# The pair stage of a graph-attention kernel: three PSUM places dealt out anew, and head scaling moved from VectorE to ScalarE and GpSimd

## What is computed

```python
alpha = jax.nn.leaky_relu(score, negative_slope=ALPHA)      # ALPHA = 0.2
m     = segment_max(alpha.T, src);  ex = exp(alpha.T - m[src])
denom = segment_sum(ex, src)[src];  att = ex / (denom + 1e-16)
out   = segment_sum(att[:, :, None] * h_e[:, dst], src)     # 8 heads of 64
x     = x + out.reshape(N, 512) + mixer(xn)
x     = x + ffn(layernorm(x))
```

## Time and profile before

| | us |
|---|---|
| median of 3 executions | 1156.71 (1156.32 to 1156.78) |
| the profiled execution | 1153.63 |
| its span, first to last instruction | 1151.5 |
| the pair stage in it, first L1873 to the first f1 matmul | 937.6 to 1096.0 |

### The profile page before, as it was taken

One profiled execution on the slowest core, in us unless ns is written; L12 is line 12 of the kernel. 1 busy time (PEld: TensorE's weight loads), 2 busy tenths in 40 slices (PEclk: granted clock), 3 DMA queues, 4 the chain that ended last, 5 costly groups with the idle time before them and its releaser, 6 DMA issues.

```text
span 1151.5 us, 11896 instructions
## 1 busy us (share of the span) xinstructions
PE 1009.2 (88%) x4204; PEld 667.0 (58%) x4204; DVE 781.3 (68%) x1315; ACT 325.8 (28%) x569; POOL 358.7 (31%) x321
## 2 busy tenths in 40 slices
PE   7779997999989998999896997999859748888988
PEld 6765487644466444844453435776546427777854
DVE  8994496534477566855434378998987659898742
ACT  5682164322310224022113111321114204333401
POOL 5371800000020102001010126777777604344400
PEclk9979995999999998999897998999989867888999
DMA  9997020020410023001120315333333295422001
GB/s 295 307 309 238 0 100 1 1 91 14 171 43 1 1 91 102 35 0 52 46 109 1 118 39 162 94 96 100 102 94 94 66 417 199 178 90 79 18 1 44
DMA packets 65314, 115.07 MB, mean 100 GB/s; under 512 B 11393, under 2 KB 43393, under 8 KB 63341
## 3 DMA queue, kind: packets, MB, share of 16 engines
q1 hardware_dynamic: 56301, 93.08, 23.7%
q0 software_dynamic: 8960, 21.31, 6.6%
HBM read 85.88 MB, written 28.49 MB: 99 GB/s over the span
## 4 chain that ended last, share of the span: by engine, by line
PE 50%; DVE 23%; POOL 11%; issue 8%; DMA 7%; ACT 0%; DVEq 0%; SPq 0%; POOLq 0%
PE ps L717 21%; PE ps L853 8%; POOL arena L657 6%; PE ps L726 5%; DMA pairs<-arena,pairi 5%; PE ps L709 4%; DVE arena L1534 4%; POOL pairs L667 4%; DVE arena L1873 3%; PE ps L751 2%; PE ps L1029 2%; DMA arena<-pairs 2%; PE ps L903 2%; PE ps L1054 2%; PE ps L789 2%
## 5 line engine op out<-in xcount | busy, mean ns | idle before, releaser
L717 PE MATMUL ps<-arena 128*125 128x512 f32 x400 | 180.2, 606 | 0.0
L586 POOL TENSOR_TENSOR small<-small 125x1 f32<-125x1 f32 x50 | 35.5, 710 | 435.5 <-DVE small L1348 435.5
L709 PE MATMUL ps<-ident,arena 125*128 125x125 f32 (+3 forms) x545 | 85.2, 298 | 51.1 <-DVE small L1873 14.2
L717 PE MATMUL ps<-arena,xnT 128*125 128x512 f32 x280 | 126.0, 608 | 4.2 <-DVE x L1786 4.2
L717 PEld LDWEIGHTS ps<-arena 128*125 128x125 f32 x400 | 75.2, 193 | 89.9 <-issue 89.9
L709 PEld LDWEIGHTS ps<-ident,arena 125*128 125x128 f32 (+3 forms) x545 | 73.7, 175 | 83.1 <-issue 37.2
L936 PE MATMUL ps<-ex_low,high 125*125 125x512 f32 x400 | 107.8, 417 | 0.0
L1212 ACT ACTIVATE arena<-ps,cols 128x125 f32<-128x125 f32 x120 | 43.2, 467 | 214.2 <-PE ps L709 214.2
L667 POOL DMA_INDIRECT pairs<-arena,pairi x80 | 87.2, 1090 | 25.5 <-issue 25.5
L717 PEld LDWEIGHTS ps<-arena,xnT 128*125 128x125 f32 x280 | 53.6, 194 | 69.7 <-issue 69.3
L692 POOL TENSOR_TENSOR arena<-arena,counts 125x625 f32<-125x625 f32 x40 | 58.0, 1452 | 105.7 <-ACT arena L1317 92.0
(11 more groups left out here) (214 smaller groups left out, 1771.5 us busy)
## 6 DMA issues: line engine op xcount, KB each, us to landing
pairs<-fill SPq DMA_DIRECT2D x10, 2500.0 KB, 22.2
arena<-pairs SPq DMA_DIRECT2D x5, 2500.0 KB, 11.2
arena<-pairs SPq DMA_DIRECT2D x10, 1250.0 KB, 6.5
arena<-in_mw SPq DMA_DIRECT2D x6, 2048.0 KB, 8.7
arena<-in_rows SPq DMA_DIRECT2D x16, 250.0 KB
arena<-in_qkv_w SPq DMA_DIRECT2D x1, 3072.0 KB
arena<-in_cw SPq DMA_DIRECT2D x3, 1024.0 KB, 5.3
arena<-in_w_qkvT SPq DMA_DIRECT2D x1, 3072.0 KB
```

The costliest lines, as they stand in the source:

```text
L709: last = pe.transpose(slot[0:n, at:at + rows], src, ident[0:rows, 0:rows])
L717: last = mm(slot[0:m, lo:hi], lhsT_of(k), rhs_of(k)[:, lo:hi], start=(k == 0), stop=(k == ks - 1))
```

## The change

Four things change, all in this stage.

- The PSUM places: scores ("pair") alternate between places 0 and 1 by head, turned rows ("exT") always take place 2. Pair n then claims what pair n-2 left, and exT n-4 what exT n-5 left.
- L1897 leaves VectorE: ScalarE scales each of the four heads by its own reciprocal in four activations of 125x64 from PSUM, at the end of its step g (after the exponential), and waits for the reciprocals.
- L1901 leaves VectorE: GpSimd adds the 256 columns to x, at the end of its step g, behind L692 of that step, and waits for ScalarE.
- VectorE does the row statistics one step later (`STATS_LAG`) and waits before them for both adds of the tile. GpSimd's power moves one step later too.

```diff
+            if name[0] == "pair":
+                at = name[2] % 2
+            elif name[0] == "exT":
+                at = 2
+            else:
+                at = k % (2 if name[0] in BESIDE_EDGES else self.SLOTS)
...
 # GpSimd, step g, behind L692
-                if g >= LAG + SUM_LAG and (g - LAG - SUM_LAG) % H == H - 1:
+                j, left = divmod(g - LAG - SUM_LAG - STATS_LAG, H)
+                if 0 <= j < NT and left == H - 1:
                     rsqrt_ln()
+                j, h = divmod(g - LAG - SUM_LAG, H)
+                if 0 <= j < NT and h % 4 == 3:
+                    b = h // 4
+                    pool.wait_ge(sig("sums_used"), 2 * j + b + 1)
+                    half = slice(256 * b, 256 * (b + 1))
+                    pool.tensor_tensor(x[:, j, half], x[:, j, half], otmp[:, half], ALU.add)\
+                        .then_inc(sig("heads_added"), 1)
...
 # ScalarE, step g, behind the exponential
-            for g in range(NT * H + LAG):
-                if g >= LAG:
+            for g in range(NT * H + LAG + SUM_LAG):
+                if LAG <= g < NT * H + LAG:
...
+                j, h = divmod(g - LAG - SUM_LAG, H)
+                if 0 <= j < NT and h % 4 == 3:
+                    b = h // 4
+                    act.wait_ge(sig("sums_inverted"), 2 * j + b + 1)
+                    if j:
+                        act.wait_ge(sig("heads_added"), 2 * (j - 1) + b + 1)
+                    for n in range(4):
+                        at = 512 * b + WIDE * n
+                        last = act.activation(otmp[:, HD * (4 * b + n):HD * (4 * b + n + 1)],
+                                              ring.psum[3][0:P, at:at + HD], ACT.Copy,
+                                              scale=rden[:, 4 * b + n:4 * b + n + 1])
+                    last.then_inc(sig("sums_used"), 1)
...
 # VectorE, step g
                     st.did(TS(r, s4[:, :, HD], 1e-16, None, ALU.add))
                     st.wait()
-                    st.did(v.reciprocal(r, r))
-                    st.wait()
-                    TT(o.rearrange("p (h e) -> p h e", h=4), s4[:, :, 0:HD],
-                       r.unsqueeze(2).to_broadcast([P, 4, HD]), ALU.mult)\
-                        .then_inc(sig("sums_used"), 1)
-                    v.wait_ge(sig("sums_used"), 2 * j + b + 1)
-                    st.did(TT(x[:, j, 256 * b:256 * (b + 1)], x[:, j, 256 * b:256 * (b + 1)], o,
-                              ALU.add))
-                    if b:
-                        st.wait()
-                        stats_of_x(j)
+                    v.reciprocal(r, r).then_inc(sig("sums_inverted"), 1)
+                j, left = divmod(g - LAG - SUM_LAG - STATS_LAG, H)
+                if 0 <= j < NT and left == H - 1:
+                    v.wait_ge(sig("heads_added"), 2 * (j + 1))
+                    stats_of_x(j)
```

More of the change, by code:

```diff
@@ L56 @@
 SUM_LAG = 2
+STATS_LAG = 1
 NORM_LAG = 3
@@ L86 @@
 BESIDE_EDGES = ("kT", "qT", "v1", "kn", "ctx", "oT", "y1", "rT")
-BESIDE_SUMS = ("pair", "exT")
 KEYS = (1, 3, 5, 7)
@@ L166, in __init__ @@
             self.nth.append((who, count[who]))
-            at = k % (2 if name[0] in BESIDE_EDGES else 3 if name[0] in BESIDE_SUMS else
-                      self.SLOTS)
+            if name[0] == "pair":
[4 more added lines that the diff above has]
+                at = k % (2 if name[0] in BESIDE_EDGES else self.SLOTS)
             self.at.append(at)
@@ L681, in _ @@
                 scatter(g, 1)
-            for g in range(NT * H + LAG + SUM_LAG):
+            for g in range(NT * H + LAG + SUM_LAG + STATS_LAG):
                 i, h = divmod(g, H)
@@ L1891, in _ @@
                         .rearrange("p (h e) -> p h e", h=4)
-                    o, r = otmp[:, 256 * b:256 * (b + 1)], rden[:, 4 * b:4 * (b + 1)]
+                    r = rden[:, 4 * b:4 * (b + 1)]
+                    if j:
+                        v.wait_ge(sig("sums_used"), 2 * (j - 1) + b + 1)
                     st.did(TS(r, s4[:, :, HD], 1e-16, None, ALU.add))
                     st.wait()
-                    st.did(v.reciprocal(r, r))
-                    st.wait()
-                    TT(o.rearrange("p (h e) -> p h e", h=4), s4[:, :, 0:HD],
-                       r.unsqueeze(2).to_broadcast([P, 4, HD]), ALU.mult)\
-                        .then_inc(sig("sums_used"), 1)
-                    v.wait_ge(sig("sums_used"), 2 * j + b + 1)
-                    st.did(TT(x[:, j, 256 * b:256 * (b + 1)], x[:, j, 256 * b:256 * (b + 1)], o,
-                              ALU.add))
-                    if b:
-                        st.wait()
-                        stats_of_x(j)
+                    v.reciprocal(r, r).then_inc(sig("sums_inverted"), 1)
[3 more added lines that the diff above has]
+                    stats_of_x(j)
                 j, left = divmod(g - LAG - SUM_LAG - NORM_LAG, H)
```

## The result

The changed kernel takes 1164.73 us (median of 20 executions, 1156.78 to 1171.39), the kernel before 1156.72 beside it (20 executions, 1149.45 to 1169.28). The ratio is 1.0061 with a 95% interval of 1.0035 to 1.0087: slower, where 1153.5 and "0.28% faster" had been predicted, and outside the range. The medians given are over all executions of a kernel; the ratios leave out those that took over 1.5% longer than its fastest, among the kernels of the experiments one of twelve in e2 and in e4 and five of twelve in e7.

What follows compares the result with a forecast made beforehand. VectorE (busy 136.6 of 158.4 us) was taken as the bound, TensorE's falling clock as a second. Terms -12.1 + 9.2 + 0.5 - 4.3 + 2.3 + 1.2 = -3.2 us took 1156.71 to 1153.5, range 1149.0 to 1158.5.

Steps and rivals of the forecast that it cites:

- (a): VectorE's blocks: without L1897 and L1901, eight of their ten pairs leave the path, a gain of 12.1 us.
- (b): VectorE before the statistics, steps 14, 22, 30, 38: new wait for GpSimd's adds, 2.3 us each, cost 9.2 us.
- (c): GpSimd's multiplications and adds running beside VectorE's work: sharing costs 0.5 us, bounds 0 and 2.0.
- (d): VectorE's waits for scores: with two places for scores 3.8 of 8.1 us remain, gain 4.3 us, bounds 0 and 8.1.
- (e): Drain after the stage's last slope: becomes one chain, longer than the former 8.0 us, cost 2.3 us, bounds 1.2 to 3.7.
- (f): Last block, from the end of the last sum to the power: 2.5 us becomes 3.7, cost 1.2 us.
- the second: Rival: VectorE's waits for scores stay, each first block making its own pause; 1157.8 us, no difference, chance 0.17.
- The slow rival: VectorE's wait for the adds is the new bound, stops of 4.1 us; 1160.7 us, slower, chance 0.13.
- the two signs that the prediction gave for being wrong: Stops above 3.1 us, or TensorE's waits for copied turned rows exceeding its former waits for VectorE and reaching VectorE.
- the first rival: TensorE's clock falls in front of the feed-forward, 3.5 us of full-clock work lost; 1157.0 us, no difference, chance 0.18.

Runs made afterwards that it cites:

- e2: The changed kernel with the old PSUM places (three taken in turn by scores and turned rows): 1158.36 us, 0.9970 of the kernel before.
- e4: The changed kernel with products nobody reads on TensorE in its pauses around the second blocks: 1154.11 us, 0.9943 of the kernel before.
- e7: e3 with 80, 40 and 12 products nobody reads on TensorE behind the scores of steps 1, 2 and 3: 1160.35 us, 0.9984 of the kernel before.
- e3: The changed kernel with GpSimd's add ahead of the multiplication of its step instead of behind it: 1145.83 us, 0.9855 of the kernel before.
- e8: The changed kernel with the statistics one more step later and the normalisation two more: 1147.10 us, 0.9878 of the kernel before.
- e9: e3 with 36, 16 and 4 products nobody reads behind the scores of steps 1, 2 and 3: 1145.09 us, 0.9868 of the kernel before.
- e1: The kernel before with only the new PSUM places for scores and turned rows: 1159.79 us, 0.9971 of the kernel before.

## Why the prediction was wrong, point by point

**(a) right.** The blocks have shrunk to 0.3 to 0.4 us, and L1897 and L1901 are gone from VectorE; its busy time in the stage fell by 12.9 us.

**(b) right in size, wrong in consequence.** Four stops of 2.15 to 2.38 us, 9.3 in all, where 4 x 2.3 = 9.2 had been worked out; the handover through GpSimd's L694 is as argued from the earlier trace rows. That the size came out so well is partly luck: L694 took 1.50 or 1.51 us in three of the four stops, where 1.29 had been taken for an idle VectorE, and the handovers 0.14 us in all in step 14, where 0.32 had been taken. The add took 0.73 us there, 0.7 had been taken. The Trainium skill ("GPSIMD Engine Reference", section "Elementwise — side-by-side cycle accounting") measures 2.6 cycles an element for two inputs; at the 1.2 GHz that it gives for GpSimd that is 0.55 us for 256 elements without the dispatch, an estimate. The 0.71 of the prediction adds 156 ns of dispatch, which the page gives for VectorE and not for GpSimd. The trace has 0.72 to 0.74 beside an idle VectorE. The add of step 9, beside a working VectorE, took 1.36.

**(c) right.** The merges average 818 ns with the adds beside them, against a median of 802 for all 40 in the same trace: 32 x 0.016 = 0.5 us, as taken. Nearly all of it is one merge, that of step 9, with 1.33 us.

**(d) is the step that failed:** a gain of 4.3 us was expected, and in the profile the waits grew by 9.7. The prediction had left 0.4 us for the start of the stage, 1.75 + 1.0 behind the first blocks, nothing behind the second ones, and 0.6 for the last tile; 4.1, 12.2 (all of it in or just behind the two stretches that begin after second blocks) and 1.5 were measured. The prediction said of the second blocks "this is ample: VectorE itself pauses some 3.7 us … and two heads lie ready when it goes on". Two heads do lie ready, but then TensorE has nothing left that it may do. It stands until VectorE reads (1.42 us) and again for the copy of the turned row (1.11), and its clock falls. That this is what costs the 12.2 us is shown by e4, where they go although the stops stay, and by e3 and e8, where they go with the stops; the 3.7 us more at the start, ahead of every stop, are not explained by it and stay open. The prediction had itself named TensorE's pauses as what lets the clock fall, and looked for them only at the first blocks, where ScalarE scales. It took 1.87 us for a length that lets the clock fall; the length alone does not decide, since 1.93 us were followed by full clock in after, e3 and e9. It also took the price of a fall from stretches of 7 to 10 us, in which VectorE still has much that is ready (6.64 busy us of 6.80 in one of them). A fall that lasts 30.7 us uses that up, and then every head waits 2.2 to 2.3 us.

**(e), (f) right but high.** From the end of the last slope (1093.45 + 0.81 = 1094.26) to 1103.72 the drain is 9.5 us, 1.5 more than in the earlier trace rows, and 2.3 were taken, of bounds 1.2 and 3.7. From 1103.72 to the power at 1107.09 it is 3.4 us, 0.9 more instead of 1.2. The four scalings took 0.93 us in the last block, with 313 ns each over the stage; 1.1 had been taken.

The sum with the measured terms, and (a) as worked out, -12.1 + 9.3 + 0.5 + 9.7 + 1.5 + 0.9 = +9.8 us, is the 9.8 by which the stage grew in the profile. With (d) alone put right it would have been 14.0 us higher, 1167.5, which is 2.8 us above the measured median: one profile is not the mean of all executions, and by the two ratios the change costs 4.3 to 7.1 us.

**The rivals.** The one that turned out nearest is the second, that the waits for scores stay as they were (1157.8): it named the waits that failed to shrink, but put their cause at ScalarE in the first blocks, and it did not go beyond 8.1 us. The slow rival named the right place, VectorE's queue behind the adds, but by a longer stop; the stop was as short as predicted, and by the ratios of e4 cost about as much through the clock as by itself. Of the two signs that the prediction gave for being wrong, stops above 3.1 us did not come. The waits of TensorE for copied rows came, with 6.6 us in total, under its former 14.2 for VectorE; it was not their total that mattered, but, as far as the traces tell, that they followed on a pause of VectorE. The clock at the feed-forward, the first rival, cost little: 3.4 us at half clock from 1097, ahead of it.

**What stays open.** The time at half clock lasts 13.7 and 30.7 us in after although TensorE hardly stands in it (30.09 of 30.70 us busy), and 10.2 or less in before. The places may cause that, since e1 shows it as well, in the slowest of its executions; what ends such a stretch no run here shows. Open too is why the first stretch of the stage, ahead of every stop, was longer in most profiles with the new places. Nor is the stop the only thing that goes before a fall: e7 shows one without it, and before has its falls behind VectorE's own blocks. And e2 shows that the stops alone, with the old places, do not make the kernel slower than before. What is shown is that without the stop such falls became rare, and that with the clock held up the waits for scores in steps 10 to 35 vanish while the stops stay.

## What to carry to other kernels

A step handed to another engine is not only priced by its own time: look where the instruction that receives it stands in that engine's queue. Moved ahead of an unrelated instruction with a wait of its own, the same add turned a loss of 0.4 to 0.6% into a gain of 1.4 to 1.5%. And when an engine that feeds on TensorE's results is made to stand, ask what TensorE may still do meanwhile: if the answer is nothing, the cost can be the pause and the slower clock behind it, which here was at least as much again (stops of 9.3 us, and 12.2 us of waits for scores, of which 1.3 were left without the stops).

## What the runs showed of the hardware

- In after, eight adds of 125x256 on GpSimd took 0.72 to 0.74 us beside a VectorE that stood, and two took 1.36 beside one that worked for all or part of the time (983.10 and 1079.37); the merge on VectorE beside the first of these took 1.33 instead of 0.80 (it began at 983.80 in the same trace).
- In after the granted clock stayed at half for 30.7 us, in which TensorE was busy for 30.09.
- TensorE's idle time of 1.93 us at the same instruction was followed by half clock in e7 and by full clock in after, e3 and e9.
- Over the 20 executions of the changed kernel the time goes with the mean granted clock listed with each: a straight line through time against time at the lower level (two times one minus the mean clock, times the span) rises by 0.34 us for each us, with a correlation of 0.85. So executions of one and the same kernel lie up to 15 us apart, and three that agree to 0.5 us say little of that.
